# A gated recurrence with two feed-forward stages on one core: gate copies on ScalarE, and the start in another order

## The reference

```python
t  = rmsnorm(x, norm1_w)
xb = causal_depthwise_conv(t @ Wx, conv_w, conv_b)           # 4 taps
r, i = sigmoid(xb @ Wa), sigmoid(xb @ Wi)
a  = exp(-8 * softplus(lam) * r)
h  = scan(h = a * h + sqrt(max(1 - a*a, 1e-12)) * (i * xb))  # along the sequence
h1 = x + (h * gelu(t @ Wy)) @ Wo
u  = rmsnorm(h1, norm2_w)
x1 = layernorm(x + h1 + (gelu(u @ Wg) * (u @ Wu)) @ Wd)
out = layernorm(x1 + relu(x1 @ W1 + b1) @ W2 + b2)
```

## Time and profile before

| | |
|---|---|
| median of 3 runs | 639.01 us |
| the profiled execution | 639.91 us |
| its span, first to last instruction | 638.0 us |
| PE busy | 606.2 us (95%) |
| DVE busy | 385.0 us (60%) |
| ACT busy | 301.6 us (47%) |
| POOL busy | 213.5 us (33%) |

### The profile page before, as it was taken

The page is one execution under the profiler, slowest core; times in us unless marked ns, Lnnn a source line. Parts: engine busy times, 40 slices in busy tenths (PEclk is TensorE's granted clock), DMA queues, the critical chain, the costliest instruction groups (busy, mean ns, idle before and its releaser), DMA issues.

```text
span 638.0 us, 9412 instructions
## 1 busy us (share of the span) xinstructions
PE 606.2 (95%) x3621; PEld 538.6 (84%) x3621; DVE 385.0 (60%) x689; ACT 301.6 (47%) x560; POOL 213.5 (33%) x309
## 2 busy tenths in 40 slices
PE   8888788899999999999999999999999999999994
PEld 7787676778988888888988888888988889988884
DVE  3984883936467563857467563856467464653544
ACT  5665513427544564437544564437544563332341
POOL 4604326411353207341353207340353205420311
PEclk9989889979999999999999999999999999999998
DMA  8600000000000100001010100001000100010010
GB/s 267 219 2 33 1 2 1 33 0 2 2 34 0 34 1 14 21 1 34 1 34 1 34 1 9 25 1 34 2 1 1 34 1 1 1 34 2 0 34 33
DMA packets 13068, 15.68 MB, mean 25 GB/s; under 512 B 584, under 2 KB 12256, under 8 KB 13024
## 3 DMA queue, kind: packets, MB, share of 16 engines
q1 hardware_dynamic: 13024, 15.09, 7.0%
HBM read 10.89 MB, written 4.19 MB: 24 GB/s over the span
## 4 chain that ended last, share of the span: by engine, by line
PE 85%; DVE 8%; POOL 3%; issue 2%; ACT 1%; DMA 1%; POOLq 0%; ACTq 0%; DVEq 0%
PE psum L280 17%; PE psum L281 17%; PE psum L282 17%; PE psum L288 10%; PE psum L290 10%; PE psum L289 10%; PE psum L295 3%; DVE xb L720 1%; DVE gu_lo L822 1%; POOL rstd L999 1%; POOL normed L1030 1%; DVE tT_lo L709 1%; DMA xs<-in_L_attn_x_dram 1%; DVE gu_raw L817 0%; DVE x1T_lo L709 0%
## 5 line engine op out<-in xcount | busy, mean ns | idle before, releaser
L1059 POOL TENSOR_SCALAR gu_hi<-gu_raw 128x512 fp32r<-128x512 f32 x64 | 50.5, 790 | 299.2 <-DVE gu_raw L817 299.2
L827 DVE TENSOR_TENSOR hid_lo<-hid_raw,hid_hi 128x512 fp32r<-128x512 f32 x64 | 45.2, 707 | 95.1 <-ACT hid_hi L603 95.1
L599 ACT ACTIVATE hid_raw<-psum,vecs 128x512 f32<-128x512 f32 x64 | 43.9, 686 | 121.3 <-PE psum L282 121.3
L817 DVE TENSOR_TENSOR gu_raw<-psum,gu_raw 128x512 f32<-128x512 f32 x64 | 44.1, 689 | 92.7 <-PE psum L282 92.7
L590 ACT ACTIVATE gu_raw<-psum 128x512 f32<-128x512 f32 x64 | 38.3, 598 | 92.3 <-PE psum L282 91.7
L288 PE MATMUL psum<-w_d_hi,gu_hi 128*128 128x256 f32 x256 | 73.0, 285 | 5.9 <-DVE w_d_lo L838 3.5
L288 PE MATMUL psum<-w_hi,hid_hi 128*128 128x256 f32 x256 | 71.7, 280 | 1.2 <-DVE hid_lo L827 0.7
L290 PE MATMUL psum<-w_d_hi,gu_lo 128*128 128x256 f32 x256 | 72.2, 282 | 0.0
L289 PE MATMUL psum<-w_d_lo,gu_hi 128*128 128x256 f32 x256 | 72.0, 281 | 0.0
L290 PE MATMUL psum<-w_hi,hid_lo 128*128 128x256 f32 x256 | 71.8, 281 | 0.0
L289 PE MATMUL psum<-w_lo,hid_hi 128*128 128x256 f32 x256 | 71.7, 280 | 0.0
(11 more groups left out here) (145 smaller groups left out, 1548.8 us busy)
## 6 DMA issues: line engine op xcount, KB each, us to landing
xs<-in_L_attn_x_dram SPq DMA_DIRECT2D x8, 512.0 KB, 3.4
out_dram<-row SPq DMA_DIRECT2D x16, 256.0 KB, 2.2
raw<-in_L_ffn_W_dram SPq DMA_DIRECT2D x2, 1024.0 KB, 13.1
raw_gud<-in_L_attn_Wg_dram SPq DMA_DIRECT2D x1, 1024.0 KB, 9.0
raw_gud<-in_L_attn_Wu_dram SPq DMA_DIRECT2D x1, 1024.0 KB, 11.1
raw_gud<-in_L_attn_Wd_dram SPq DMA_DIRECT2D x1, 1024.0 KB, 13.2
raw_xyai<-in_L_attn_Wx_dram SPq DMA_DIRECT2D x1, 256.0 KB, 2.7
raw_xyai<-in_L_attn_Wy_dram SPq DMA_DIRECT2D x1, 256.0 KB, 3.1
```

The costliest lines, as they stand in the source:

```text
L599: nc.scalar.activation(hid_raw[:, w % SLOTS, :], bank[:, :], ACT.Relu, bias=vec("b1", m)).then_inc(relu_ready, 1)
L817: nc.vector.tensor_tensor(gu_raw[:, r % SLOTS, :], up_bank(r)[:, :], gu_raw[:, r % SLOTS, :], ALU.mult).then_inc(gu_ready, 1)
L827: nc.vector.tensor_tensor(hid_lo[:, w % SLOTS, :], hid_raw[:, w % SLOTS, :], hid_hi[:, w % SLOTS, :].bitcast(FP32), ALU.subtract).then_inc ...
L1059: nc.gpsimd.tensor_scalar(gu_hi[:, r % SLOTS, :], gu_raw[:, r % SLOTS, :], 1.0, 0.0, ALU.mult, ALU.add).then_inc(gu_hi_ready, 1)
```

## The change

1. `gate_hi` moves from GpSimd to ScalarE, in all 64 rounds, right behind `gelu_gate(r)`. It still waits for `gate_times_up(r)`.
2. The GpSimd splits of W1 and W2 in rounds 0 to 3 become ScalarE splits in rounds 1 and 3.
3. `square_h1` (m = 6) on ScalarE goes ahead of `gelu_gate`.
4. The adding of b2 on GpSimd (`add_b2`) goes from ahead of the copy at m = 2 to behind `ln_scale` at m = 3.
5. VectorE, front: the steps for `half_c` go from behind the split of chunk 1's t to ahead of the split of chunk 0's t. The low half of Wd goes from round 0 to ahead of round 0; those of W1 and W2 move by one or two rounds; `scan_both(1)` goes behind `gate_lo(3)`; at m = 7 the split of u goes ahead of `gate_lo`; in period 1 the last convolution step goes behind the split of x1.
6. GpSimd splits of Wg, Wu, Wd wait for chunk 0's low half of xb (`xb_lo_ready`), no longer for its convolution.
7. TensorE: `mlp_down` of the last chunk writes to the `DOWN` banks and so waits for `s1_ready`, not `s2_ready`; in round 66 `mlp_down(55)` goes ahead of `mlp_up(56)`; `keep_running(18)` becomes 24.

```diff
@@ tensor
-                if m == 0 and c >= 1:
+                if m == 0 and c == CHUNKS - 1:
+                    pe.wait_ge(s1_ready, 2 * CHUNKS)
+                elif m == 0 and c >= 1:
                     pe.wait_ge(s2_ready, 2 * c)
...
+                if r == UNITS + 2:
+                    mlp_down(r - LAG_DOWN)
                 if units(r - LAG_UP):
                     mlp_up(r - LAG_UP)
-                if units(r - LAG_DOWN):
+                if units(r - LAG_DOWN) and r != UNITS + 2:
                     mlp_down(r - LAG_DOWN)
...
-            keep_running(18, SECOND)
+            keep_running(24, SECOND)
@@ scalar
+            def gate_hi(r):
+                act.wait_ge(gu_ready, r + 1)
+                if r >= SLOTS:
+                    act.wait_ge(d_done, r - SLOTS + 1)
+                nc.scalar.activation(gu_hi[:, r % SLOTS, :], gu_raw[:, r % SLOTS, :],
+                                     ACT.Copy).then_inc(gu_hi_ready, 1)
...
+                if mixing and m == 6:
+                    square_h1(n)
                 if units(r):
                     gelu_gate(r)
+                    gate_hi(r)
                 if mixing and p == 0:
...
+                    if m == 1:
+                        weight_hi("1")
+                    if m == 3:
+                        weight_hi("2")
@@ vector
-                if r == 3:
-                    scan_both(n)
...
-                if r == 0:
-                    weight_lo("d")
...
+                if r == 3:
+                    scan_both(n)
...
+                if m == 2 and p == 1:
+                    convolve(n, 2)
@@ gpsimd
-                if m == 2 and first:
-                    add_b2(f)
-                if r < UNITS:
-                    gate_hi(r)
-                if r < 2:
-                    weight_hi("1", ks=[r])
-                elif r < 4:
-                    weight_hi("2", ks=[r - 2])
...
+                if m == 3 and first:
+                    add_b2(f)
```

More of the change, by code:

```diff
@@ L138, in up_bank, with second_bank @@
             return psum[SECOND + 1] if r < KH and r % 2 else psum[UP]
+        def second_bank(c):
+            return DOWN if c == CHUNKS - 1 else SECOND
         vecs_loaded = sem("vecs_loaded")
@@ L414, in mlp_down @@
                 pe.wait_ge(hid_lo_ready, w + 1)
-                if m == 0 and c >= 1:
+                if m == 0 and c == CHUNKS - 1:
+                    pe.wait_ge(s1_ready, 2 * CHUNKS)
+                elif m == 0 and c >= 1:
                     pe.wait_ge(s2_ready, 2 * c)
                 for tt in range(TT):
-                    last = product_by_tokens(half_bank(SECOND, tt), "2", m, hid_hi[:, w % SLOTS, toks(tt)],
+                    last = product_by_tokens(half_bank(second_bank(c), tt), "2", m, hid_hi[:, w % SLOTS, toks(tt)],
                                              hid_lo[:, w % SLOTS, toks(tt)], m == 0 and tt % 2 == 0, m == KH - 1)
@@ L653, in round_of @@
                 if mixing:
-                    if m == 6:
-                        square_h1(n)
                     if m == 7:
@@ L811, in second_sum @@
                     total = pair_of(rows[c % 2], q)
-                    nc.vector.tensor_tensor(total, psum[SECOND + q][:, :], total, ALU.add).then_inc(s2_ready, 1)
+                    nc.vector.tensor_tensor(total, psum[second_bank(c) + q][:, :], total,
+                                            ALU.add).then_inc(s2_ready, 1)
             def gate_times_up(r):
@@ L864, in first_period @@
                     hy_lo(n)
-                gate_lo(r)
-                if r == 0:
-                    weight_lo("d")
[L868 to L875, removed]
                 if r == 7:
                     split_lo(uT_lo, uT_hi, uT_hi_ready, uT_lo_ready, n)
+                gate_lo(r)
+                if r == 2:
+                    weight_lo("1", ks=[0])
+                if r == 3:
+                    scan_both(n)
+                if r == 4:
+                    weight_lo("1", ks=[1])
+                if r == 5:
+                    weight_lo("2", ks=[0])
+                if r == 6:
+                    weight_lo("2", ks=[1])
             def round_of(r):
@@ L911, in round_of @@
                         hy_lo(n)
+                    if m == 7:
+                        split_lo(uT_lo, uT_hi, uT_hi_ready, uT_lo_ready, n)
                 if m == 3 and second:
@@ L918, in round_of @@
                         convolve(n, 1)
-                        convolve(n, 2)
+                        if p > 1:
+                            convolve(n, 2)
                     if m == 4:
                         room(n)
-                    if m == 7:
-                        split_lo(uT_lo, uT_hi, uT_hi_ready, uT_lo_ready, n)
                 if m == 0 and first:
@@ L944, in _ @@
             weight_lo("x", "n1")
[L945 to L952, removed]
             lams = vecs[:, VECS["lam"]:VECS["lam"] + KD]
@@ L968, in _ @@
                                            ALU.add).then_inc(consts_ready, 1)
+            split_lo(tT_lo, tT_hi, tT_hi_ready, tT_lo_ready, 0)
+            weight_lo("y", "n1")
+            weight_lo("a")
+            weight_lo("i")
+            for step in range(LOOKBACK):
+                convolve(0, step)
+            xb_lo(0)
+            split_lo(tT_lo, tT_hi, tT_hi_ready, tT_lo_ready, 1)
             weight_lo("g", "n2")
@@ L986, in _ @@
             split_lo(uT_lo, uT_hi, uT_hi_ready, uT_lo_ready, 0)
+            weight_lo("d")
             for r in range(KH):
@@ L1053, in add_b2 @@
                                             ALU.add).then_inc(b2_added, 1)
[L1055 to L1060, removed]
             def weight_hi(n, norm=None, ks=None):
@@ L1116, in _ @@
             tail(0)
-            pool.wait_ge(taps_added, 3 * KD)
+            pool.wait_ge(xb_lo_ready, KD)
             weight_hi("g", "n2")
```

## The result

The changed kernel takes 651.13 us (median of 4 runs, 650.24 to 652.84) against 639.04 us (4 runs): ratio 1.0194, 95% interval 1.0167 to 1.022. It is slower, as forecast, and by the amount forecast (651).

What follows compares the result with a forecast made beforehand. TensorE was taken as the bound, fully busy from 302 to 600 us. Terms +17.7 - 3.1 - 2.2 + 0.4 - 0.6 = +12.2 on the 639.01 median gave 651.2, stated as 651; overall range 643 to 659.

Steps and rivals of the forecast that it cites:

- Part 1: Periods 1 to 6: gate_hi on ScalarE delays mlp_up and mix_out, 2.95 us a period, +17.7 us in all.
- The absorbed case: Rival, steady part: ScalarE's detour is absorbed, no steady loss, the gains alone stand, 633.5 us; chance 0.12.
- the half case: Rival, steady part: ScalarE catches up between copy and root, only 1 us a period lost, 639.5 us; chance 0.09.
- The clock case: Rival: the two new waits lower the clock in every period, 10 us more, 661 us; chance 0.11.
- Part 2: Front up to round 0: mix_out of chunk 0 starts 1.6 earlier, clock holds for 1.5 more; -3.1 us (-1 to -4.5).
- Part 3: Period 0: idle time only changes place, part of the slow clock's 3.4 us is won; -2.2 us (0 to -4).
- The stretch behind it: Round 8 to first mlp_up: mix_x 0.7 later, VectorE -0.3, the 3.3 us mlp_up wait stays; net +0.4 us.
- Part 4: Tail: mlp_down(57) then waits on VectorE; what remains of the 0.6 us wait goes, -0.6 us (0 to -1.3).

Runs made afterwards that it cites:

- e3: Changed kernel with gate_hi on GpSimd only at m = 4 and 5 of periods 1 to 6 (12 of 64 rounds): 632.15 us, ratio 0.9904.
- e4: Changed kernel with gate_hi on GpSimd only at m = 4 of periods 1 to 6: 638.77 us, ratio 0.999.
- e8: Changed kernel, gate_hi still on ScalarE but in periods 1 to 6 behind square_decay (m = 4) and gelu_y (m = 5): 634.80 us.
- e1: Kernel before the change with one edit, gate_hi on ScalarE right behind gelu_gate in all 64 rounds: 653.15 us, ratio 1.0231.
- f4: Changed kernel with TensorE's tail as before (old banks, s2_ready, mlp_down(55) behind mlp_up(56)): 651.73 us, one run.
- f3: e2 with the 15 steps for half_c back behind the split of chunk 1's t: 628.42 us, ratio 0.9813.
- f6: e2 with the half_c steps behind the low halves of Wa and Wi, and b2 early for the last chunk: 626.47 us.
- e2: Changed kernel with every gate_hi copy back on GpSimd: 626.63 us, ratio 0.982.

## Why the prediction was right, and where it was not

**Part 1, the steady loss: right in mechanism, place and size.** Predicted 2.95 us a period and 17.7 in all; the two waits with their restarts make 3.0, the steady period went from 71.81 to 74.83 us, and the six periods together lost 17.2, the first of them less for the reason given below the table. The chain behind the copy was to come 2.19 us later, and the load did (2.81 us behind the start of the gelu instead of 0.62). The slack of 0.30 us at `mlp_up` and of nearly nothing at `mix_out` was read from the rows of before. e3 shows that the loss lies in these two places together, e4 separates them, and e8 shows the slack: a root one copy later costs 0.23 us. What the profile offered for this was not a busy share (ScalarE went from 47% to 53%) but an in-order row with a wait in front of work that had none.

**The absorbed case and the half case fell**: VectorE idles the same 1.25 us before the scan, only later. **The clock case fell** in all traces: with waits of 1.60 and 0.88 us the window from 302 to 600 has a clock of 1.00, in e1 and f4 too.

**Part 2, the front: near in size, 2.68 us against 3.1, but half of it was not the change.** The sum gave 1.5 us to the clock at `mix_out` of chunk 0, which was to hold once the wait of 2.04 us was gone. e1 has the front of the kernel before, waited 2.01 us there, and kept a clock of 1.00; f3 waited 2.95 and kept it too. So a wait of 2 us there does not always bring the slow matmuls of the earlier trace rows, and that removing it saves them was not shown. e1 begins round 0 at 58.19 us: 1.28 of the 2.68 are the clock, and the moves themselves gave 1.4, for which the prediction had 1.6 (`mix_out` began 1.16 us earlier; of the terms behind the 1.6, the 0.3 stands on no row).

The chain for `half_c` ran from 7.53 to 12.27, and the first product came 1.6 us late (1.3 predicted). The seven steps that took 1.34 us in quiet took 2.73 beside GpSimd:

```profile
8.95 2.73 DVE L979 SCALAR_TENSOR_TENSOR sp<-sp 128x2 f32<-128x2 f32 x7
```

This is what the SBUF — State Buffer page of the Trainium skill ("Who interferes with whom") states of two SBUF inputs beside a GpSimd instruction that reads SBUF, and the trace agrees. The 0.99 us step, which the prediction took for a case of it, has one input. But the trace of before has two steps with two inputs among the others, and each ends within 0.02 us of the end of a GpSimd split (25.75 and 26.77 us):

```profile
24.91 0.85 DVE L960 TENSOR_TENSOR sp<-sp 128x2 f32<-128x2 f32 x1
25.79 0.98 DVE L961 TENSOR_TENSOR sp<-sp 128x2 f32<-128x2 f32 x1
```

The price is not a fixed one: in f6 six of the seven steps ran while GpSimd wrote `normed`, and the seven took 1.62 us.

**Part 3, period 0: the clock mis-sized, 2.2 predicted, 4.38 in this profile.** The waits came to 6.9 us instead of 8.6: the splits of W1 and W2 take 1.99 us for both pieces of one weight on ScalarE, not 2.3. And the clock did not fall at all in period 0 of this execution. In f4, the same code up to the tail, it did, and the period took 46.64 us. The predicted 46.2 lies between them. e1, with none of the moves for this period but the copy, took 44.20, so the 4.38 can't be put down to the new order of item 5.

**The stretch behind it: wrong in sign.** I had +0.4 and it was -0.58. The wait of 3.3 us at the first `mlp_up`, which I held to stay, fell to 1.9 (2.8 in e1, 1.2 in e2); which of the moves did it, no run isolates.

**Part 4, the tail: wrong.** The step read "-0.6 (bounds 0 and -1.3)", and it was +0.8: +0.4 from the transposes of the last x1 on and +0.4 in period 7. At `mlp_down(57)` 0.6 were won (9.87 us behind the transposes instead of 10.51), but `mlp_down(58)` was already 0.2 late (13.49 instead of 13.29). What I had missed is `add_b2` of the last two chunks: I had followed its move in period 1, and not in the rounds in which nothing else hides it. With it early again for chunk 7, in f6, the tail is 0.4 us shorter than before the change.

**The sum.** Terms by prediction: +17.7 - 3.1 - 2.2 + 0.4 - 0.6 = +12.2. In the spans: +17.2 - 2.7 - 4.4 - 0.6 + 0.8 = +10.4 (rounded); in the medians: +12.1. The profiled execution of the changed kernel (650.24) was its fastest, and the one of the kernel before (639.91) lies above its median; how much slow clock an execution has in its first 160 us is worth more than the error of the sum, so the forecast of that part was not tested to 1 us.

## What to carry to other kernels

Before moving an operation to an emptier engine, list what is queued behind it there, and what it waits for: a 0.6 us copy cost 3.0 us a period, because its wait stood ahead of a chain with 0.3 us of slack, and put behind the first half of that chain on the same engine it cost 0.23. Where an edit joins several moves, run the one part that repeats most by itself: with all copies on GpSimd the other moves win 12 to 13 us, and the copies on ScalarE cost some 24. And follow a moved operation through the first and the last period too, where its cover is gone.

## What the runs showed of the hardware

**The same wait does not always bring the clock down.** e3 and e4 are the same program up to round 12. In both, TensorE waits 2.18 us at 69.1. The 13th matmul behind it, and then the row at the same place of the other:

```profile
70.64 0.40 PE L288 MATMUL psum<-uT_hi,w_g_hi 128*128 128x512 f32 x1
```

```profile
70.69 0.63 PE L288 MATMUL psum<-uT_hi,w_g_hi 128*128 128x512 f32 x1
```

The second (e4) is at the lower level, and stays there until about 73.9. So a stretch with such waits has a time of its own in each execution; differences of 1 to 3 us in the front of one profile say little, and the stretches behind it should be compared by themselves.

**A table switch right behind another function showed no time but the load here either**: behind the copy, the load starts 0.02 us after it (290.13 + 0.64 against 290.79), and the exponential 0.01 us after the load.
